# GpSimd takes the floors of four pair units, and unit 13 is counted without marks

## The reference, cut to what matters

```python
h = jnp.maximum(_layernorm(x, axis=-1), 0.0)
support = h @ weight                          # 4096 x 64
mask = (adj != 0).astype(support.dtype)       # 4096 x 4096, about 16 neighbours in a row
rank = jnp.cumsum(mask, axis=1)
deg = rank[:, -1:]
k = jnp.minimum(deg, float(MAX_NEIGH))        # 100
pos = rank - (deg - k)
w = mask * jnp.where(pos > 0, DECAY ** (k - pos), 0.0)   # DECAY 0.5
return x + (w @ support + bias)
```

## Time and profile before

| what | us |
|---|---|
| median of 3 runs | 217.07 (216.46 to 217.47) |
| the profiled execution: its own time | 217.53 |
| the profiled execution: span | 215.0 |
| busy PE / DVE / ACT / POOL | 196.2 / 196.9 / 160.4 / 33.2 |

### The profile page before, as it was taken

The page is one execution under the profiler, slowest core; times in us unless marked ns, Lnnn a source line. Parts: engine busy times, 40 slices in busy tenths (PEclk is TensorE's granted clock), DMA queues, the critical chain, the costliest instruction groups (busy, mean ns, idle before and its releaser), DMA issues.

```text
span 215.0 us, 6506 instructions
## 1 busy us (share of the span) xinstructions
PE 196.2 (91%) x2784; PEld 187.7 (87%) x2784; DVE 196.9 (92%) x239; ACT 160.4 (75%) x303; POOL 33.2 (15%) x52
## 2 busy tenths in 40 slices
PE   0288889899899999999999999999999999999993
PEld 0277567798797999999989999999999999999993
DVE  0999978896989999999999999999999999999893
ACT  2351996685697888788777878788988989998720
POOL 8700010050000004050102141500000000000000
PEclk9999999999999999999999999999999999999998
DMA  6999999999999999999999999999998100000001
GB/s 219 193 215 193 202 218 216 213 218 212 218 213 218 212 217 215 218 211 220 215 218 218 213 218 213 220 215 219 217 213 180 26 0 3 15 12 3 17 0 43
DMA packets 7675, 36.12 MB, mean 168 GB/s; under 512 B 1632, under 2 KB 3424, under 8 KB 3424
## 3 DMA queue, kind: packets, MB, share of 16 engines
q0 software_dynamic: 4608, 33.56, 75.2%
q1 hardware_dynamic: 2880, 2.13, 3.7%
q10 hardware_dynamic: 160, 0.03, 0.1%
HBM read 68.22 MB, written 1.05 MB: 322 GB/s over the span
## 4 chain that ended last, share of the span: by engine, by line
PE 78%; DMA 12%; DVE 3%; POOL 3%; ACT 2%; issue 1%; POOLq 0%
PE acc L634 38%; PE chain L627 24%; PE chain L625 14%; DMA adj_b<-in_adj 12%; ACT powers L317 2%; PE chain L613 2%; DVE masks L363 1%; DVE part L369 1%; POOL adj_b L249 1%; POOL sums L263 1%; DVE later L404 1%; DVE sums L369 0%; POOL sums L264 0%; POOL ident_f L260 0%; DVE sum_b L446 0%
## 5 line engine op out<-in xcount | busy, mean ns | idle before, releaser
L317 ACT ACTIVATE powers<-chain 128x512 int16<-128x512 f32 (+1 forms) x279 | 148.3, 573 | 35.3 <-PE chain L627 34.0
L634 PE MATMUL acc<-support,powers 128*128 128x192 bf16 x1024 | 160.0, 246 | 2.5 <-ACT powers L317 2.4
L627 PE MATMUL chain<-diag_own,masks 128*128 128x128 bf16 x608 | 106.7, 219 | 0.0
L625 PE MATMUL chain<-diag_past,masks 128*128 128x128 bf16 x568 | 102.0, 219 | 1.3 <-ACT powers L317 0.9
L634 PEld LDWEIGHTS acc<-support,powers 128*128 128x128 bf16 x1024 | 95.9, 98 | 6.4 <-issue 4.7
L363 DVE TENSOR_SCALAR masks<-adj_b 128x4096 uint8<-128x4096 bf16 x32 | 72.7, 2282 | 5.1 <-DMA adj_b<-in_adj 5.1
L627 PE MATMUL chain<-diag_step,masks 128*128 128x128 bf16 x416 | 60.2, 219 | 0.0
L627 PEld LDWEIGHTS chain<-diag_own,masks 128*128 128x128 fp8e3 x608 | 59.5, 99 | 0.2
L625 PEld LDWEIGHTS chain<-diag_past,masks 128*128 128x128 fp8e3 x568 | 55.7, 99 | 3.5 <-ACT powers L317 2.3
L249 POOL DMA_DIRECT2D adj_b<-in_adj x32 | 28.7, 902 | 105.7 <-DVE masks L363 105.0
L627 PEld LDWEIGHTS chain<-diag_step,masks 128*128 128x128 fp8e3 x416 | 39.6, 99 | 0.0
(11 more groups left out here) (49 smaller groups left out, 65.4 us busy)
## 6 DMA issues: line engine op xcount, KB each, us to landing
adj_b<-in_adj POOLq DMA_DIRECT2D x32, 1024.0 KB, 35.3
x_sb<-in_x SPq DMA_DIRECT2D x1, 1024.0 KB, 4.8
out<-x_sb SPq DMA_DIRECT2D x14, 64.0 KB, 5.8
out<-x_sb SPq DMA_DIRECT2D x4, 32.0 KB, 9.0
w<-in_L_gnn_weight ACTq DMA_DIRECT2D x2, 16.0 KB, 5.9
bias_b<-in_L_gnn_bias SPq DMA_DIRECT2D x1, 32.0 KB, 9.5
```

The lines of the kernel that those rows point to most:

```text
L317: nc.scalar.activation(powers[:, c, b, cols].bitcast(i16), chain[c][:, cols], ACT.Relu, bias=(MAX_NEIGH + 1) * STEP).then_inc(powers_ready ...
L625: nc.tensor.matmul(chain[c][:, at:at + P], column(n, t + 1), diag_past[:, :], start=False, stop=False, skip_group_check=True)
L627: return nc.tensor.matmul(chain[c][:, at:at + P], column(n, t), diag_own[:, :] if marked else diag_step[:, :], start=False, stop=True, ski ...
L634: return nc.tensor.matmul(acc[u % ACCS][:, k * 3 * D:(k + 1) * 3 * D], powers[:, u % FLIGHT, s + 1 if k < MARKS[u] else s, at:at + P], sup ...
```

## The change

`MARKS` of unit 13 goes from 2 to 0. The floors of units 13 to 16 are issued by GpSimd behind its last load, each once ScalarE has finished the batch's powers, with semaphores of their own; VectorE's differences wait for them. Where the units' differences now stand without a floor of VectorE between them, each waits for the one before. `STARTS`, `LAGS` and everything else stay.

```diff
-    MARKS = [1, 1, 1, 2, 2, 0, 2, 2, 0, 2, 2, 0, 2, 2, 0, 0, 0, 0]
+    MARKS = [1, 1, 1, 2, 2, 0, 2, 2, 0, 2, 2, 0, 2, 0, 0, 0, 0, 0]
+    POOL_UNITS = (13, 14, 15, 16)
 ...
     def floors_until(u):
-        return sum(len(to_floor(v)) for v in range(u % FLIGHT, u, FLIGHT))
+        return sum(len(to_floor(v)) for v in range(u % FLIGHT, u, FLIGHT)
+                   if (v in POOL_UNITS) == (u in POOL_UNITS))
 ...
             for n in range(4, NT):
                 load(n)
+            def floor(u, j):
+                c = u % FLIGHT
+                last = BATCH[u] * (j + 1)
+                pool.wait_ge(powers_ready[c], taken_until(u) + last + 1)
+                bits = powers[:, c, first_of(u, j):last + 1, plain(u)].bitcast(i16)
+                nc.gpsimd.tensor_scalar(bits, bits, STEP, None, ALU.max).then_inc(pool_floored[c], 1)
+            for g in range(SLOTS):
+                for u in POOL_UNITS:
+                    if (g - STARTS[u] - 1) % BATCH[u] == 0 and (g - STARTS[u] - 1) // BATCH[u] - 1 in to_floor(u):
+                        floor(u, (g - STARTS[u] - 1) // BATCH[u] - 1)
 ...
                 if done:
-                    dve.wait_ge(floored[c], done)
+                    dve.wait_ge(pool_floored[c] if u in POOL_UNITS else floored[c], done)
+                if j and u in POOL_UNITS:
+                    dve.wait_ge(weights_ready[c], batches_until(u) + j)
 ...
                 for u in range(NU):
-                    if (g - STARTS[u] - 1) % BATCH[u] == 0 and (g - STARTS[u] - 1) // BATCH[u] - 1 in to_floor(u):
+                    if u not in POOL_UNITS and (g - STARTS[u] - 1) % BATCH[u] == 0 and (g - STARTS[u] - 1) // BATCH[u] - 1 in to_floor(u):
                         floor(u, (g - STARTS[u] - 1) // BATCH[u] - 1)
```

More of the change, by code:

```diff
@@ L182, in gnn_decay_kernel @@
         floored = [sem(f"floored{c}") for c in range(FLIGHT)]
+        pool_floored = [sem(f"pool_floored{c}") for c in range(FLIGHT)]
         weights_ready = [sem(f"weights_ready{c}") for c in range(FLIGHT)]
```

## The result

The changed kernel took 284.27 us (median of 4 runs, 281.69 to 286.35) against 217.10 before: a ratio of 1.3068, 95% interval 1.3024 to 1.3113. One of the four runs, 286.35, fell in a slower state of the core and is not in the ratio. The direction and the mechanism of the forecast hold, its size does not: 239 was forecast, at most 253. The profiled execution took 285.41 us, 67.9 more than the one before.

A forecast was written before the change was run, and what follows sets the result against it. PE and VectorE were taken as full from 158.9 us. GpSimd's 31 us plus 4.5 of differences less 7.6 of floors gave +27.9, less overlap and slack +22.5: 239 us forecast, range 216.5 to 253.

The forecast's parts named there:

- What bounds the kernel: From 158.9 us PE and VectorE both full; VectorE's scans just in time for PE, 0.53 us to spare at unit 15.
- PE's saving: Unit 13 without its second count: 60 matmuls fewer on PE in slots 76 to 90, worth 3.3 us.
- the term for unit 17: Unit 17's scans end 1.26 us later, after one more difference and further floors removed, inside their 1.94 us to spare.
- The gates: Unit 13's differences delay VectorE's scans, making PE's base matmuls 0.6 (unit 15) and 0.25 us (unit 16) late: +0.3 us.
- GpSimd's floors: 16 floors, 34,816 elements a partition, on GpSimd: 31 us at a memset's rate, 57 at a select's; 31 was taken.
- Full exclusion: From 158.9 us VectorE and GpSimd take turns, never running masks, floors or two-SBUF-input instructions together: 239 us, chance 0.48.
- my sum: Full exclusion's added GpSimd and VectorE work, less idle time, overlapping additions and end slack: +22.5 us, 240.0 for the profiled execution.
- What would show it: Signs: GpSimd floors above 1.8 us, longer VectorE instructions, engines waiting, PE's busy share from 160 us falling to some 70%.
- Exclusion only against masks and VectorE's own floors: Rival: GpSimd's floors hold up only VectorE's masks and floors, three masks ahead of unit 16's scans: 220.5 us, chance 0.12.
- No exclusion: Rivals: engines share no path; GpSimd at 0.84 ns an element 217.4 us, chance 0.2; at 1.6 ns 222, chance 0.06.
- PE's saving reaches the end: Rival: no exclusion and VectorE's scans in time, so the 3.3 us fewer matmuls shorten the kernel: 214 us, chance 0.14.

The follow-up runs named there:

- run 1: Changed kernel with the floors of units 13 to 16 left out altogether, on GpSimd and VectorE, as if GpSimd cost nothing: 217.74 us, ratio 1.0055.
- run 3: Changed kernel with all floors on VectorE and none on GpSimd, unit 13 still without marks: 224.24 us, ratio 1.0328.
- run 10: Kernel before, with no floors in any unit and unit 13 without marks: 214.66 us, ratio 0.9891.
- run 7: Kernel before, plus eleven instruction forms on GpSimd alone behind the last store, with nothing else running: one run, 261.44 us.
- run 5: Kernel before, plus 8 extra floors on GpSimd on an unused load buffer, for which nobody waits: 253.02 us, ratio 1.1677.
- Free: Another name for run 1, the changed kernel without any floors in units 13 to 16: 217.74 us, ratio 1.0055.
- run 6: Kernel before, plus 24 write-only GpSimd memsets on an unused load buffer, three in place of each extra floor of run 5: 234.47 us, ratio 1.0820.

## Why the prediction was wrong in size

- **What bounds the kernel: right.** VectorE was as full as PE, with 0.53 us to spare at unit 15. Runs 1, 3 and 10 show that this decides whether PE's saving arrives. One slip, which changes nothing: the term for unit 17 says three floors and rightly takes off four (0.73 + 3 x 0.60).
- **The gates: right, one missed.** +0.3 us forecast, +1.1 measured (run 1); the two scans came as late as worked out, the additions were not in the sum.
- **GpSimd's floors: the step that failed.** "I take 31" us, and 57 as the other end; measured 95.1. All the figures named for them, 31, 52 and 57 us, were too low. The nearest rows were a memset, which does not read or compute, and a select of 128 elements. Neither bounds a tensor-scalar from above: alone it takes 5.36 us for 2048 elements (run 7). At that rate the 16 floors take some 91 us with nothing beside them (an estimate, 12 x 5.36 + 4 x 6.65), so nearly all of the 95.1 is GpSimd's own. The range's upper end came from the same two rows, and so missed too.
- **Full exclusion: right in kind, too strong in degree.** With 95 in place of 31 my sum would give 240 + 64 = 304 us for the profiled execution, which took 285.4. The difference goes the way of run 5: an instruction with two inputs gets its turn before GpSimd's floor ends. Free has the same instructions as the changed kernel but for GpSimd's floors, and its span is 68.2 us shorter (215.3 against 283.5). VectorE is busy 250.9 us in the one and 194.0 in the other: 56.9 us of the 68.2 are instructions that take longer. Set beside the median of their kind in free, those that overlap a floor of GpSimd are 56.7 us longer, and all others together are no longer at all. The other 11.3 us are idle time: VectorE waits 14.4 us for floors of GpSimd, and a little less for others. So some 24 of the floors' 95.1 us cost VectorE nothing (95.1 - 56.9 - 14.4, an estimate), 1.5 us for each floor, where full exclusion has none.
- **What would show it: found, though not in size.** Floors above 1.8 us, masks, scans and differences longer, VectorE waiting for GpSimd and PE for scans and differences: all are there. PE's busy share from 160 us on fell to 54% (66.9 of 123 us), not 70.

The busy times in the changed kernel and in free:

```profile
PE 209.6 (74%) x2724; PEld 197.7 (70%) x2724; DVE 250.9 (89%) x231; ACT 161.1 (57%) x304; POOL 128.4 (45%) x68
```
```profile
PE 193.5 (90%) x2724; PEld 184.2 (86%) x2724; DVE 194.0 (90%) x231; ACT 160.4 (74%) x304; POOL 31.2 (14%) x52
```

- **The rivals.** "Exclusion only against masks and VectorE's own floors" is what a writing GpSimd does (run 6), not a reading one. "No exclusion" in either form is out by run 5. "PE's saving reaches the end" comes true only where VectorE loses work ahead of the scans of units 15 and 16 (run 10); with the floors of units 13 to 16 gone for nothing it did not (run 1).
- The Trainium skill's rule ("SBUF — State Buffer", "Who interferes with whom") fits all three signs: masks and floors shut out by reads and writes (runs 5, 6), tensor-tensors by reads alone. That the second "fully blocks" holds for masks and floors; for a tensor-tensor run 5 shows its turn over 1.45 us before the floor's end.

Not settled: how much of the loss is PE's lower clock. It was granted only behind stretches in which PE waited, and no run held it up. The two pages bound its direct part: PE is busy 209.6 us in place of 193.5 with the same 2724 matmuls, so 16.1 of the 68.2 us at most are slower matmuls; the other 52.1 us PE stands idle.

## What to carry to other kernels

Work moved from a full VectorE to GpSimd does not leave VectorE: in this kernel each floor that cost VectorE 0.6 us cost the kernel 3.7 to 4.5 us on GpSimd, even when nobody waited for it (4.5 us, run 5). Before such a move, take the instruction's time from a row of the same operation on the same engine, not from a memset; if there is none, the range's upper end is open. And when two engines are full, check the deadlines that the one sets the other, one by one, before counting a saving: PE's 3.3 us were worth nothing in run 1. They arrived, most of them, where VectorE dropped its floors altogether (run 10, 1.1% faster), at the price of leaving the floor out.

## What the runs showed of the hardware

- GpSimd alone (run 7), 2048 elements a partition: tensor-scalar 5.36 us in int16, bf16 and fp32 alike; tensor-tensor product in bf16 4.05, with two inputs and still faster; copy 1.89; memset 1.80.
- Beside GpSimd's floors VectorE's masks, floors, scans, sums and differences are held up, beside its memsets only the masks and floors (runs 5, 6). It works the other way too: the floor of GpSimd that was asked for at 202.18 in run 5, under the mask that ran until 204.16, took 7.19 us in place of 5.36.
- A VectorE instruction that is held up so is recorded as busy: a 0.42 us sum as 3.73 us (run 5). Where the changed kernel's VectorE is 100% busy with three instructions in 10 us, most of it is waiting.
